# A fused adaLN transformer block: eight modulation-weight slices in eight buffers at once, or two at a time through two buffers

## The reference, cut to what matters

```python
mod = (_silu(L0_c) @ L0_wmod).reshape(L0_c.shape[0], 6, 1, -1)
sa, ca, ga, sb, cb, gb = (mod[:, 0], mod[:, 1], mod[:, 2], mod[:, 3], mod[:, 4], mod[:, 5])
ga = (2 * (ga >= 0) - 1) * jnp.maximum(jnp.abs(ga), 0.25)
gb = (2 * (gb >= 0) - 1) * jnp.maximum(jnp.abs(gb), 0.25)
h = _layernorm(x, axis=-1) * (1 + ca) + sa
x = x + ga * _L0_attn_ref(h, L0_attn_wq, L0_attn_wk, L0_attn_wv, L0_attn_wo)
h = _layernorm(x, axis=-1) * (1 + cb) + sb
x = x + gb * _L0_ffn_ref(h, L0_ffn_gate_w, L0_ffn_lora_A, L0_ffn_lora_B)
```

## Time and profile before

| | |
|---|---|
| median of 3 runs | 2666.47 us (2665.12 to 2667.07) |
| the profiled execution's own time | 2667.07 us |
| its span (first to last instruction) | 2665.3 us |
| TensorE busy | 2602.6 us, 98% |
| VectorE busy | 1594.9 us, 60% |
| ScalarE busy | 1154.2 us, 43% |
| GpSimd busy | 250.5 us, 9% |
| mean granted TensorE clock | 0.993 of full speed |
| moved by DMA | 499.78 MB, mean 188 GB/s |

### The profile page before, as it was taken

How to read it: one execution, slowest core, us unless ns; L and a number is a source line. 1 busy time by engine, 2 the same in 40 slices (tenths; PEclk the granted TensorE clock), 3 DMA queues, 4 the chain that set the end, 5 groups by cost and what they waited for, 6 DMA issues and landing times.

```text
span 2665.3 us, 40308 instructions
## 1 busy us (share of the span) xinstructions
PE 2602.6 (98%) x12873; PEld 2158.9 (81%) x12873; DVE 1594.9 (60%) x4151; ACT 1154.2 (43%) x2582; POOL 250.5 (9%) x120
## 2 busy tenths in 40 slices
PE   5999999999999999999999999999999999998999
PEld 3778787888888888888888888888888888886887
DVE  3766666666766565556656665556566665546553
ACT  3555555454344443333444443333444443335441
POOL 2323333332000000000000000000000000000122
PEclk8999999999999999999999999999999999999999
DMA  7667755558654444435545543347455555546221
GB/s 279 257 218 260 259 201 199 193 196 321 230 181 148 140 160 159 157 143 217 194 173 181 181 151 125 131 153 280 180 179 198 212 189 221 186 167 243 100 80 56
DMA packets 175640, 499.78 MB, mean 188 GB/s; under 512 B 15088, under 2 KB 57392, under 8 KB 174000
## 3 DMA queue, kind: packets, MB, share of 16 engines
q1 hardware_dynamic: 170352, 479.61, 49.8%
q10 hardware_dynamic: 5184, 18.88, 1.8%
HBM read 376.76 MB, written 121.67 MB: 187 GB/s over the span
## 4 chain that ended last, share of the span: by engine, by line
PE 76%; issue 15%; POOL 6%; DVE 1%; DMA 1%; ACT 1%; SPq 0%; POOLq 0%; DVEq 0%; ACTq 0%
PE bank L632 23%; PE bank L634 23%; PE bank L633 23%; PE bank L697 4%; POOL w_q_lo L602 3%; POOL w_o_lo L602 2%; DMA stage<-in_wv 1%; POOL w_k_lo L602 1%; PE bank L1638 0%; PE bank L248 0%; PE bank L725 0%; DVE rotated L1050 0%; POOL w_v_lo L602 0%; DMA wm<-in_wmod 0%; PE bank L1651 0%
## 5 line engine op out<-in xcount | busy, mean ns | idle before, releaser
L632 PE MATMUL bank<-w_o_hi,qo_hi 128*128 128x512 f32 x1024 | 409.2, 400 | 0.9 <-DVE acc L1067 0.7
L632 PE MATMUL bank<-hT_hi,w_q_hi 128*128 128x512 f32 x1024 | 400.8, 391 | 0.2 <-DVE swapped L1047 0.2
L634 PE MATMUL bank<-w_o_hi,qo_lo 128*128 128x512 f32 x1024 | 399.9, 391 | 0.0
L633 PE MATMUL bank<-w_o_lo,qo_hi 128*128 128x512 f32 x1024 | 398.8, 389 | 0.0
L634 PE MATMUL bank<-hT_hi,w_q_lo 128*128 128x512 f32 x1024 | 398.7, 389 | 0.0
L633 PE MATMUL bank<-hT_lo,w_q_hi 128*128 128x512 f32 x1024 | 398.7, 389 | 0.0
L874 ACT ACTIVATE prob<-prob,nbias 128x384 f32<-128x384 f32 (+2 forms) x512 | 273.5, 534 | 130.6 <-DVE nbias L1080 119.9
L1080 DVE CUSTOM_DVE_ANT_0 prob<-bank,mask_t 128x384 f32<-128x384 f32 (+2 forms) x512 | 231.2, 453 | 144.8 <-PE bank L634 92.0
L1046 DVE TENSOR_TENSOR rotated<-bank,cos_t 128x512 f32<-128x512 f32 x160 | 110.6, 691 | 310.5 <-ACT swapped L858 308.4
L951 ACT ACTIVATE pT_hi<-bank 128x384 fp32r<-128x384 f32 (+2 forms) x512 | 203.8, 405 | 185.0 <-PE bank L697 179.6
L1067 DVE TENSOR_TENSOR acc<-bank,acc 128x512 f32<-128x512 f32 x256 | 173.8, 688 | 182.1 <-PE bank L634 182.1
(11 more groups left out here) (207 smaller groups left out, 4772.6 us busy)
## 6 DMA issues: line engine op xcount, KB each, us to landing
w_q_hi<-w_q_hi_scratch SPq DMA_DIRECT2D x96, 512.0 KB, 8.2
w_q_lo<-w_q_lo_scratch SPq DMA_DIRECT2D x96, 512.0 KB, 8.9
w_o_hi<-w_o_hi_scratch SPq DMA_DIRECT2D x96, 512.0 KB, 7.8
w_o_lo<-w_o_lo_scratch SPq DMA_DIRECT2D x96, 512.0 KB, 8.4
stage<-in_wq SPq DMA_DIRECT2D x32, 512.0 KB, 5.2
stage<-in_wo SPq DMA_DIRECT2D x32, 512.0 KB, 5.3
w_q_hi_scratch<-w_q_hi SPq DMA_DIRECT2D x32, 512.0 KB, 6.4
w_q_lo_scratch<-w_q_lo SPq DMA_DIRECT2D x32, 512.0 KB, 7.1
```

Of the source, the lines that this page charges most:

```text
L632: eng.matmul(o, st[0], mv_[0], start=start, stop=False)
L633: eng.matmul(o, st[0], mv_[1], start=False, stop=False)
L634: return eng.matmul(o, st[1], mv_[0], start=False, stop=stop)
```

## The change

The eight buffers become two: slices go alternately to `stage[0]` and `stage[1]`, with a semaphore each. SyncE may load slice c of the run of 24 once slice c-2 has been multiplied (it waits on `s_mm1`). Slices 0 and 1 of a part are requested at the head of the group's queue, ahead of w_q; 2 and 3 after w_k; 4 and 5 ahead of the first w_o chunk; 6 ahead of the third and 7 ahead of the fourth. TensorE multiplies slice 0 after output half 5, slice 1 after half 7, slices 2 and 3 after the steps k = 3 and k = 7 of Q0, 4 and 5 likewise in Q1, and 6 and 7 in Q2. The matmuls, their order of summation and their number stay as they are, and so do bytes and count of the loads. `lx`, `l_hi`, `l_lo`, `r_hi`, `r_lo` are not used by the parts any more; `lf` still holds their result.

```diff
-        part_rows = [stage[0][:], stage[1][:], lx[:]] + [t[:].bitcast(F32).rearrange("p k n -> p (k n)") for t in (l_hi, l_lo, r_hi, r_lo)] \
-            + [lf[:].rearrange("p k n -> p (k n)")]
...
-        s_dv = sem("s_dv"); s_dk = sem("s_dk"); s_do = sem("s_do"); s_vk = sem("s_vk"); s_lw = sem("s_lw")
+        s_dv = sem("s_dv"); s_dk = sem("s_dk"); s_do = sem("s_do"); s_vk = sem("s_vk"); s_lw = [sem("s_lw0"), sem("s_lw1")]
...
-        def sp_direct_group(eng, n, before_o=None):
+        def sp_direct_group(eng, n, before_o=None, with_o=lambda j: None):
...
             for j in range(6, NC):
+                with_o(j)
                 sp_fetch(eng, j, n % KV, s_do)
 
-        def sp_part(eng, q, n):
-
-            eng.wait_ge(s_pv, QT * n)
-            for k in range(KT):
-                eng.dma_start(part_rows[k], late_source(KT * q + k)).then_inc(s_lw, 16)
+        def sp_part_slices(eng, q, ks):
+
+            for k in ks:
+                i = KT * q + k
+                c = i - KT
+                if c >= 2:
+                    eng.wait_ge(s_mm1, i - 1)
+                eng.dma_start(stage[c % 2][:], late_source(i)).then_inc(s_lw[c % 2], 16)
...
-                    sp_direct_group(eng, n, lambda: sp_part(eng, q, n))
+                    sp_part_slices(eng, q, (0, 1))
+                    sp_direct_group(eng, b * KV + g, lambda: sp_part_slices(eng, q, (2, 3)),
+                                    lambda j: sp_part_slices(eng, q, {6: (4, 5), 8: (6,), 9: (7,)}.get(j, ())))
...
-        def pe_part(eng, q):
-
-            eng.wait_ge(s_lw, 16 * KT * q)
-            for k in range(KT):
-                pe_slice(eng, KT * q + k, part_rows[k])
+        def pe_part_slice(eng, i):
+
+            c = i - KT
+            eng.wait_ge(s_lw[c % 2], 16 * (c // 2 + 1))
+            pe_slice(eng, i, stage[c % 2][:])
...
-                    if part is not None and h == 1 and k == KT - 1:
-                        pe_part(eng, part)
+                    if part is not None and h < 3 and k % 4 == 3:
+                        pe_part_slice(eng, KT * part + 2 + 2 * h + k // 4)
...
                         pe_wo(eng, n - 1, half, True, True)
+                        if half % 2:
+                            pe_part_slice(eng, KT * q + (half - FILL) // 2)
                     pe_qv(eng, n, True, part=q)
```

More of the change, by code:

```diff
@@ L523, in sp_groups @@
                 for g in range(1 + QT, KV):
-                    n = b * KV + g
                     q = g - QT
-                    sp_direct_group(eng, n, lambda: sp_part(eng, q, n))
+                    sp_part_slices(eng, q, (0, 1))
+                    sp_direct_group(eng, b * KV + g, lambda: sp_part_slices(eng, q, (2, 3)),
+                                    lambda j: sp_part_slices(eng, q, {6: (4, 5), 8: (6,), 9: (7,)}.get(j, ())))
                     if q == 1:
```

## The result

The changed kernel takes 2682.19 us (median of 5 runs, 2678.28 to 2682.72) against 2666.47 us before (5 runs, 2665.12 to 2667.22): a ratio of 1.006, 95% interval 1.005 to 1.0072. That is 15.7 us slower, as was forecast in sign; the forecast was 12.5 us, the range reached to 19.5. The profiled execution took 2682.8 us, span 2681.0, which is 15.7 us over the profiled one of before.

What follows compares the result with a forecast made beforehand. TensorE's stream was taken as the bound. Excursions +8.5 us and waits +4.5 us gave +13.0 us, 2679.5 against the median of 2666.47, stated as 2679.0 us (+0.47%); range 2672.5 to 2686 us, 8 times in 10.

Steps and rivals of the forecast that it cites:

- What bounds the kernel: In the changed groups TensorE's own stream sets the time, with 2.6 us of waits; spreading the load burst gains nothing.
- The excursions: TensorE's visits to narrow slice matmuls: three bunches at 3.81 us become 24 lone slices at 0.83 us, net +8.5 us.
- the value by the bunch: Lone slice's cost on TensorE, taken from the bunch of eight less seven slices at 0.43 us: 0.80 us.
- that by the pair: Lone slice's cost on TensorE, taken from a pair's 1.26 us less one slice of 0.43 us: 0.83 us, the one used.
- Slices 2 to 5 and the other covers: Loads of slices 2 to 5 at least 2.4 us early; w_o, w_q, w_v and ScalarE's copy covered: cost 0.
- Slices 6 and 7: TensorE waits 0.95 and 0.55 us for slices queued behind w_o loads: 1.5 us a part, 4.5 us for three.
- Rival 1: At slices 6 and 7: both arrive in time, so only excursions cost, +8.5 us, 2675.0 us; chance 0.25.
- ring order: On SyncE's queue, slice 6 can't overtake the four w_o loads before it; without this the 4.5 us of waits would be 0.
- The discount: At late slices: 2679.5 lowered to 2679.0 us, because an arrival just late may hide in the excursion's drain.
- the forecast's own range: Whole kernel: excursions plus waits from +10.5 to +17.5 us, given as 2676.4 to 2684 us.
- Rival 2: At lone slices on TensorE: each overlaps the wide matmuls and costs 0.48 us, kernel unchanged at 2666.5 us; chance 0.12.
- Rival 3: At the two buffers: lone loads take 8 us, so slices 3 to 5 are late too, +9 us more, 2688; chance 0.08.

Runs made afterwards that it cites:

- run 1: Changed kernel with all eight slice loads of a part requested ahead of the eight w_o loads: 2673.37 us, ratio 1.0027.
- run 2: Kernel before, eight buffers and one burst of loads kept, but slices multiplied singly at the changed kernel's places: 2674.3 us, ratio 1.0027.
- run 3: Changed kernel with slice loads ahead of w_o and slices multiplied in pairs, 12 excursions instead of 24: 2670.01 us, ratio 1.0011.
- run 4: Changed kernel with slice loads ahead of w_o, each slice's four narrow matmuls replaced by one full-width matmul by the identity: 2668.17 us, ratio 1.0003.
- run 9: Changed kernel with slices 6 and 7 requested on ScalarE's queue, third and fourth w_o chunks held back as in the changed kernel: 2687.77 us, ratio 1.0077.
- run 7: Changed kernel with slice 6 requested behind six w_o loads instead of four, together with slice 7: 2696.11 us, ratio 1.0107.
- run 5: Kernel before, with TensorE also waiting for all eight w_o loads ahead of each bunch of slices: 2684.99 us, ratio 1.0067.
- run 6: Kernel before, with TensorE waiting ahead of each bunch for the first three w_o chunks only: 2673.19 us, ratio 1.0026.

## Why the prediction held, and where it was off

*What bounds the kernel.* Right. TensorE's stream sets the time, and every microsecond put into it came out: in runs 1 to 3 the profile's own excursions account for the medians within 1 us. Nothing was gained from the burst that went.

*The excursions.* Forecast +8.5 us, from 0.83 us for a lone slice. Measured 0.79, so +7.5 us in the trace, and +6.6 by the medians of run 1. The mechanism was right and the size slightly off: the value by the bunch, 0.80, was nearer than that by the pair, since the second slice of a pair costs 0.45 and not 0.43. That the price is mostly one of changing the tile (about 0.30 of 0.36 us) is shown by run 4 with the weight loads at the edges; that the engine drains there is what the Trainium skill says (TensorEngine Tiling (Array Packing), section Tiling Modes) and not something that a row shows.

*Slices 2 to 5 and the other covers.* Right: no waits there in any part, none for w_o, and w_q and w_v are in time, none for the bank that ScalarE copies out late.

*Slices 6 and 7.* The place was right, the size was not: forecast 0.95 and 0.55 us in each part, 4.5 us in all. Measured were 2.57, 1.23 and 1.86 us for slice 6 and none, 0.35 and 0.25 for slice 7, 6.3 in all. The sum has two terms, the landing of slice 5 and eight loads at the pace of a full queue, and in its total it was the first that was mis-sized. Slice 5 was to land 3.9 us after its request (7.1 to 11.0; by the 3.7 us of its own row the waits would be 1.3 us a part and not 1.5). It took 4.5, 3.9 and 5.5 us in parts 1, 2 and 3; the issue of part 3:

```profile
stage<-in_wmod SPq DMA_DIRECT2D x1, 512.0 KB, 5.5
```

Slices 2 to 4 took 3.5 to 3.9 us in all three parts; only slice 5 has w_o loads requested right behind it. In run 1 these stand behind slice 7, and there slices 5 and 6 landed after 3.5 to 4.0 us and slice 7 after 4.3 to 4.4. So in five of these six parts the load with w_o requested right behind it landed later than the others, which the sum did not price. From its landing to that of slice 6, five loads, went 1.59, 1.44 and 1.24 us a load, and to that of slice 7, eight loads, 1.48, 1.39 and 1.26: 1.38 in the mean, against 1.37 in the sum. In part 1 the sum had both the landing and the pace too fast, in part 2 only the pace up to slice 6, and in part 3 only the landing, while there its pace was too slow. The 0.7 us more in the mean landing of slice 5 make 2.2 us over three parts, against 1.8 that were missing. In part 1 slice 7 was not waited for because the low clock had held TensorE back.

Rival 1, no waits at all, needed a slice 6 that lands earlier and got a later one; run 1 is its case with the order changed, and came within 2 us of its 2675.0. The cause as put, ring order, is not what decides: by run 9 the slice waits about as long in another ring. What is shown is that it lands late when requested behind four w_o loads with the engines full (share 1.02 while TensorE waits), and that two loads more ahead of it cost 2.1 to 2.6 us (run 7). How the chip lets a second ring in was not settled.

*The discount.* 0.5 us were taken off because an arrival just late might hide in the excursion. It did not: the two excursions behind waits of 0.35 and 0.25 us cost 1.20 and 1.12 us by the six steps behind each: the 0.79, all of the wait and 0.06 to 0.08 besides. The lower end of the forecast's own range is also mis-added: 10.5 us above the median of 2666.47 are 2677.0 and not 2676.4.

*What was missing.* The clock. The forecast had a wait cost its length; behind the wait of 2.57 us came 1.6 us of matmuls at half pace. The kernel before shows the like, outside the stretch whose waits the prediction read (TensorE in order of time):

```profile
2449.07 0.61 PE L1651 MATMUL bank<-h_hi,gT 128*16 128x512 f32 x1 [3.15 <-DVE h_lo L1518]
2449.47 0.63 PE L1652 MATMUL bank<-h_lo,gT 128*16 128x512 f32 x1
```

Behind this wait of 3.15 us the matmuls start 0.43 us apart and the granted clock is 0.50 from 2449 to 2452; behind one of 3.41 us, at 87.10, it is 0.50 from 87 to 90. Of the waits ahead of slices, over all runs, eleven were of 2.17 us and longer, and the low clock stood behind ten of them, not behind one of 2.26 us (run 9); it stood behind none of 2.03 us or less. A wait of 2.17 us with it and one of 2.26 us without: the length alone does not decide. Runs 5 and 6 show in the kernel before that it goes with the wait and not with the slices.

*How the total came out.* Measured +15.7 us, forecast +12.5. The excursions were put 1.0 us too high, the waits 1.8 too low, 0.5 were taken off that should not have been, and the 1.6 of the clock were in no term. Nothing in the working made room for the last; that the range held it too is luck.

*Rival 2*, a lone slice that hides in the stream, decides from 0.70 us downwards; at 0.79 it did not come. *Rival 3* did not come either: slice 5, the last of the lone loads, was at no time waited for, though in part 3 it landed only 0.8 us ahead of TensorE instead of at least 2.4.

Left open: one of the five runs took 2678.28 us and the others 2681.5 to 2682.7; of all 25 executions of the changed kernel two took 2678.3 to 2678.6 and the others 2681.3 or more. A faster w_o, and with it a shorter wait without the low clock, could make about that, but no profile caught it. None of the versions tried beats the kernel before; it has three excursions, and fewer would give at most 0.37 us for each one less.

## What to carry to other kernels

When one engine's stream is the bound, work that needs another tiling of TensorE is best done in few and long excursions: here 0.36 us for each visit besides 0.43 us for each slice, so cutting three visits into 24 cost 7.5 us by the trace and 6.6 to 7.6 by the medians of runs 1 and 2. Fewer buffers are free only if each refill is requested ahead of bulk loads that nobody waits for yet; moving the last two slice loads of a part ahead of w_o took all the waits away. And price a new wait of TensorE of over 2 us at its length plus what the lower clock takes behind it, and look through the whole trace, not only the stretch that changes, for waits that already show it.

## What the runs showed of the hardware that had not been expected

A TensorE wait of 2.2 to 2.9 us, with full-speed work on both sides, was followed in all but one case by matmuls at half pace, costing 1.5 to 2.9 us; after 3.9 to 5.0 us and a lone slice it was 2.5 us. One full-width float32 matmul of 256 columns between the split matmuls costs 0.49 us, while four narrow ones of 256 columns each cost 0.79, and the weight load at either edge of the narrow ones does not run ahead of its matmul as the others do. And a load issued on an idle queue (run 9, slice 6 of part 1) moved no byte for 3.4 us while another engine's loads, issued before it, filled the DMA engines; a load with nothing right behind it landed in 3.5 to 3.9 us altogether.
